# Order of rope products and of maxima blocks at a batch boundary of an attention and soft-MoE layer

## The reference

```python
h = _layernorm(x, axis=-1) * (1 + ca) + sa
x = x + ga * _L0_attn_ref(h, Wq, Wk, Wv, Wo)      # rope(q), rope(k), causal softmax
h = _layernorm(x, axis=-1) * (1 + cb) + sb
x = x + gb * _L0_ffn_ref(h, ...)
# in _L0_ffn_ref:
dispatch = jax.nn.softmax(logits, axis=1)          # over tokens
combine = jax.nn.softmax(logits.reshape(b, n, e * s), axis=-1)
slots = jnp.einsum('bnd,bnes->besd', xn, dispatch)
# two expert matmuls with a gelu between them, giving eo
out = jnp.einsum('bmd,bnm->bnd', eo, combine)
```

## Time and profile before

| | us |
|---|---|
| median of 3 runs | 3299.77 (3297.85 to 3300.67) |
| the profiled execution, device time | 3297.0 |
| its span, first to last instruction | 3295.2 |
| PE busy | 3071.7 (93%) |
| DVE busy | 2252.1 (68%) |
| ACT busy | 1763.6 (54%) |
| POOL busy | 329.8 (10%) |
| TensorE's granted clock, mean | 0.981 |

### The profile page before, as it was taken

How to read it: one execution, slowest core, us unless ns; L and a number is a source line. 1 busy time by engine, 2 the same in 40 slices (tenths; PEclk the granted TensorE clock), 3 DMA queues, 4 the chain that set the end, 5 groups by cost and what they waited for, 6 DMA issues and landing times.

```text
span 3295.2 us, 45435 instructions
## 1 busy us (share of the span) xinstructions
PE 3071.7 (93%) x17679; PEld 1544.8 (47%) x17679; DVE 2252.1 (68%) x4403; ACT 1763.6 (54%) x3199; POOL 329.8 (10%) x193
## 2 busy tenths in 40 slices
PE   5799999999889999998989999999997999999899
PEld 2433334447553333453854333344575433334468
DVE  4788887562678888756368888856546888885632
ACT  2366666564236666645514666654540566665560
POOL 3200000210400000111130000012122000002200
PEclk9799999999999999999999999999999999999999
DMA  4322201015502220002542202000443220100052
GB/s 129 99 40 40 40 2 39 14 52 197 149 20 40 40 40 27 20 7 95 190 119 46 39 9 40 27 20 7 151 163 103 40 41 11 31 27 27 9 179 81
DMA packets 123555, 201.89 MB, mean 61 GB/s; under 512 B 10094, under 2 KB 106996, under 8 KB 120232
## 3 DMA queue, kind: packets, MB, share of 16 engines
q1 hardware_dynamic: 110820, 148.58, 13.9%
q10 hardware_dynamic: 12520, 50.40, 8.2%
HBM read 156.01 MB, written 42.16 MB: 60 GB/s over the span
## 4 chain that ended last, share of the span: by engine, by line
PE 74%; DVE 17%; ACT 4%; issue 2%; POOL 1%; DMA 1%; ACTq 0%; SPq 0%; DVEq 0%; POOLq 0%
PE ps L694 14%; DVE pm L1269 12%; PE ps L674 10%; PE ps L614 9%; PE ps L795 7%; PE ps L850 7%; PE ps L627 6%; PE ps L881 3%; PE ps L870 3%; PE ps L574 2%; PE ps L738 2%; PE ps L659 2%; PE ps L678 1%; PE ps L808 1%; PE ps L603 1%
## 5 line engine op out<-in xcount | busy, mean ns | idle before, releaser
L1269 DVE TENSOR_REDUCE pm<-ps 128x1 f32<-128x512 f32 (+4 forms) x2560 | 1376.9, 602 | 273.6 <-PE ps L614 181.9
L983 ACT ACTIVATE R<-ps 128x512 f32<-128x512 f32 (+1 forms) x2240 | 1175.5, 593 | 603.0 <-PE ps L674 412.1
L674 PE MATMUL ps<-R 99*128 99x512 bf16 (+3 forms) x2560 | 827.9, 349 | 10.7 <-ACT R L983 6.0
L614 PE MATMUL ps<-R 96*128 96x512 bf16 x1536 | 578.6, 387 | 46.2 <-DVE pm L1269 40.7
L694 PE MATMUL ps<-R 128*17 128x512 f32 (+3 forms) x5120 | 528.9, 531 | 0.0
L614 PEld LDWEIGHTS ps<-R 96*128 96x128 bf16 x1536 | 147.3, 97 | 446.4 <-DVE pm L1269 372.0
L674 PEld LDWEIGHTS ps<-R 99*128 99x128 bf16 x2560 | 241.4, 97 | 146.0 <-ACT R L983 64.1
L694 PEld LDWEIGHTS ps<-R 128*17 128x17 f32 x5120 | 117.8, 96 | 280.1 <-issue 168.3
L850 PE MATMUL ps<-R 128*128 128x512 f32 x512 | 231.7, 610 | 14.0 <-ACT R L1050 13.9
L627 PE MATMUL ps<-R 128*128 128x257 f32 x1024 | 237.4, 388 | 4.1 <-ACT R L934 3.6
L795 PE MATMUL ps<-snT,R 128*128 128x512 f32 x512 | 230.1, 593 | 0.0
(11 more groups left out here) (151 smaller groups left out, 3321.7 us busy)
## 6 DMA issues: line engine op xcount, KB each, us to landing
R<-in_L_ffn_w_dram SPq DMA_DIRECT2D x64, 1024.0 KB, 5.8
R<-q_parts ACTq DMA_DIRECT2D x12, 768.0 KB
R<-k_parts ACTq DMA_DIRECT2D x12, 768.0 KB
R<-in_L_attn_x_dram SPq DMA_DIRECT2D x16, 512.0 KB, 8.4
q_parts<-R SPq DMA_DIRECT2D x16, 512.0 KB, 3.6
k_parts<-R SPq DMA_DIRECT2D x16, 512.0 KB, 3.4
R<-in_L_attn_x_dram SPq DMA_DIRECT2D x4, 2048.0 KB, 8.3
x_park<-R SPq DMA_DIRECT2D x16, 512.0 KB, 2.6
```

The lines of the kernel that those rows point to most:

```text
L614: last = mm(ps[:, bank, :], qt(4 * c + r), kt(4 * kc, 4), start=True, stop=True)
L674: last = mm(bank[:, i * w:(i + 1) * w], kst[g % 2][0:BROWS, h0 + i, j * P:(j + 1) * P], qst[g % 2][0:BROWS, h0 + i, (c + 1) * CH - w:(c + ...
L983: A(Eb[s % ESLOTS][:, h0:h0 + n, 0:w], ps[:, u % NST, 0:n * w].rearrange("p (n w) -> p n w", n=n), ACT.Exp, scale=SCALE).then_inc(s_ex, 1)
L1269: mx = lambda o, i: V.tensor_reduce(o, i, AX.X, ALU.max)
```

## The change

In `combine` on PE, a block now stands behind the expert products e = 0, 2, 4 and 6 of a tile, as many as the tile has, up to four; a fifth block stays behind the tile. `blocks_in_tile(n)` gives their numbers. On DVE the reductions of those blocks stand ahead of `out_tile(n)`, the fifth behind it; remainder 7 stays behind output tile 7. In the rope loop DVE's `products(b + 1, i)` moves ahead of `out_tile(i - 2)` and `remainder(b + 1, i - 1)`. The instructions themselves, their number and their operands stay the same.

```diff
--- before.py
+++ after.py
@@ -101,6 +101,11 @@
 
 def early_by(n):
     return EARLY * (n + 1 - FIRST_WITH_MAXES) // (NT - FIRST_WITH_MAXES)
+
+
+def blocks_in_tile(n):
+
+    return range(early_by(n - 1), min(early_by(n), early_by(n - 1) + E // 2)) if n >= FIRST_WITH_MAXES else range(0)
 
 
 def values_by(i):
@@ -626,7 +631,10 @@
                 for e in range(E):
                     last = mm(ps[:, 6 + n % 2, 0:D + 1], EcT[:, e, n * P:(n + 1) * P], eo[:, e, :],
                               start=e == 0, stop=e == E - 1)
-                last.then_inc(s_cm, 1)
+                    if e == E - 1:
+                        last.then_inc(s_cm, 1)
+                    elif b + 1 < B and e % 2 == 0 and e // 2 < len(blocks_in_tile(n)):
+                        max_unit(b + 1, blocks_in_tile(n)[e // 2])
 
             for c in range(NC):
                 turn_xhat(0, c)
@@ -903,6 +911,7 @@
                     m = 0
                     for n in range(QU - 2, NT):
                         combine(b, n)
+                        m += len(blocks_in_tile(n))
                         while m < early_by(n):
                             max_unit(b + 1, m)
                             m += 1
@@ -1526,14 +1535,17 @@
                     products(b + 1, 1)
                     remainder(b + 1, 0)
                     for i in range(2, QU):
+                        products(b + 1, i)
                         out_tile(i - 2)
                         remainder(b + 1, i - 1)
-                        products(b + 1, i)
                     m = 0
                     for n in range(QU - 2, NT):
+                        for m in blocks_in_tile(n):
+                            reduce_unit(b + 1, m)
                         out_tile(n)
                         if n == QU - 1:
                             remainder(b + 1, QU - 1)
+                        m = max(early_by(n - 1), 0) + len(blocks_in_tile(n))
                         while m < early_by(n):
                             reduce_unit(b + 1, m)
                             m += 1
```

## The result

The changed kernel takes 3240.8 us (median of 4 runs, 3237.0 to 3244.1) where the kernel before, run beside it, takes 3300.0 (3297.9 to 3300.7). The ratio is 0.9827, with an interval of 0.9815 to 0.9839: 59 us less. The forecast was 3240 us.

The account below looks back on a forecast made before the run. At three batch boundaries PE mostly waits for DVE; 0.5 + 9 x 3.47 + 9.6 + 1.0 + 0.5 + 1.4 = 44.2 us each saves 60.0 us, 3297.0 to 3237, median 3240 us. Forecast range 3230 to 3246 (0.66); 8 in 10: 3226 to 3262.

Parts of the forecast that it names:

- 44.2 us a stretch: Each batch boundary, combine tile 7's start to first `values` matmul: 44.2 us forecast, against 63.68, 64.21 and 64.69 before.
- Rope order: Rope units at the boundaries: products run at PE's pace, 6.92 us; products 7 end at 875.2, ending PE's 2.69 us wait.
- The term behind it: Combine tile 7 waits for output tile 5, now behind products 7, until 876.5: 0.5 us a boundary.
- Combine tiles and blocks: PE's work from combine 7 on: nine tiles of 3.47 us, 9.6 us of blocks, plus 1.0 us a boundary for insertions.
- The second rival: Blocks inserted within tiles show their weight loads, 0.29 us each, 31 us back: 3271 us, or 3255 for half; chance 0.09.
- DVE stays under PE: In the boundary stretch DVE has some 38.3 us of work against PE's 41 to 42.
- The 0.5 us that I took for tile 8: In tile 8 the fourth block waits for a reduction that stands behind remainder 7: 0.5 us a boundary.
- The first rival: DVE becomes the bound and PE waits inside tiles 7 to 10: 2 to 4 us a boundary, 3246 to 3252 us; chance 0.13.
- The end: `values` 0 waits for output tile 15, now behind four reductions and the tile's last matmul: 1.4 us a boundary.
- Full clock: Whole boundary stretch at 2.4 GHz, granted clock 1.00 instead of 0.92, since the two long PE waits are gone.
- What follows moves up whole: After the boundary, `values`, scores and maxima keep their order; their loads are issued some ten microseconds or more early.
- The slower rival: Park loop: late parks hold products at DVE's head; binds from 4.3 us landing, 3305 to 3310 us at 14; chance 0.04.

Follow-up runs that it names:

- after_third: The changed kernel run unaltered once more, as the reference beside the last variants: 3239.7 us, 0.9822 against the kernel before.
- both_waits: Changed kernel, but first `values` matmuls wait only for output tile 14, second group for 15, and output tile 5 precedes products 7 on DVE: 3232.3 us.
- after_again: The changed kernel run unaltered again beside other variants: 3239.7 us, 0.9830 against the kernel before.
- rope_only: Kernel before with only products moved ahead of output tile and remainder on DVE; blocks and reductions as before: 3283.4 us, 0.9961.
- order_only: Changed kernel with its rope and DVE order, but PE's blocks stand behind the tile again, as before: 3256.7 us, 0.9880 against the kernel before.

## Why the prediction was right

It named the place, the mechanism and the size: 44.2 us a stretch against 44.45 measured, 60.0 us in all against 59. That the stretch agrees to 0.25 us is in part luck: one term was 0.7 us too small and another 0.5 too large, as follows.

- Rope order: right. Products run at 6.91 us, products 7 are done at 876.1, which is 875.2 counted from combine tile 0 of the kernel before, and their wait is gone. The term behind it was too small: combine 7 waits for output tile 5 until 878.24 and not until 877.5 by the same clock, 1.2 us with latency against 0.5. The prediction let that tile end 1.3 us after products 7 (875.2 to 876.5), which is about what it takes alone (1.06 by the earlier trace rows) and a latency; by the 1.65 us that the prediction itself gives for a tile beside POOL the term would have been 0.8 or more. Here it ends 2.1 us after them, since its last step takes 1.44 us beside POOL's rotate. The stretch of 43.7 us in after_third, where it took 0.42, shows that it is this step.
- Combine tiles and blocks, 31.2 and 9.6 us: right. both_waits has no wait and takes 41.79 us, so 0.94 us are left over for the 36 insertions, 26 ns each if all of it is theirs. 1.0 was taken. The tiles take 4.5 to 4.9 us, where 4.3 to 4.8 were forecast. The second rival, weight loads in the open at 0.29 us, falls with its reason: if both loads were in the open, the full block of 0.22 us would take 0.5. By the rule of the Trainium skill (TensorE: Matmul & The Clock Gate, "Part 3: Packing small matmuls — row/col tiling") that the prediction cites, a weight load overlaps running matmuls only for other rows of the array; this trace does not agree, as the load at 894.87 shows. The same section also lets a load for the background weight buffer be pulled ahead, without that condition; whether these loads go there the profile doesn't show.
- DVE stays under PE: right. The 0.5 us that I took for tile 8 did not come; PE waits for no reduction. The first rival would have shown waits of L608 to L619 inside the tiles; there are none in tiles 7 to 15. DVE is busy for 38.7 us of the stretch (38.3 forecast), though a remainder beside POOL takes 2.28 us and not 2.06.
- The end, 1.4 us: 1.18 of wait and 0.2 of latency.
- Full clock: right, 1.00 in all three stretches.
- What follows moves up whole: right; from `values` 0 to the next logits 470.4 us after and 470.6 before, in batch 1.
- The slower rival: its loop is as described, 11.72 us a unit at two sets, and at three it costs nothing, as forecast. But it stands nearer to binding than the 2.1 us of slack that the prediction gave it: the landing of 2.2 us was read from one park, and for unit 2 it is 3.4 to 3.6 us in the changed kernel's profile. At the third boundary of after_again it is 4.3 us, and products 5 come 0.1 us late (2433.13, 7.04 behind products 4); at that of after_third it is 4.5, and they come 0.4 late. The prediction's 4.3 us, from which the loop would bind, agrees with that.

Where I was wrong was in the expectations of the parts. For the rope order alone I gave 24 us and measured 13: the first reduction still comes 1.7 us later than I had reckoned, since the remainder that was moved back stands in its way, and I took the low clock to vanish with a shorter wait. In the whole change neither matters, because blocks and reductions stand ahead of these and no long wait is left. The sum was right for the whole; the share that I gave the rope order was not.

## What to carry to other kernels

Where two engines take turns in tiles, look at what the second one does while the first works on the tile: here DVE waited 2.2 us a tile for its end with reductions at hand that needed only a few matmuls, and it was enough to put small pieces of work between the matmuls of a long accumulation, at some 26 ns each here, and their consumers ahead of the tile's own. Put the instruction that starts another engine's chain ahead of the one that waits for that chain's end, and check the buffers' loop first, with the slowest landing in the trace and not one row's: with one set fewer the same order was slower than the kernel before. The gains of the two parts alone (13.4 and 36.6 us) did not add up to the whole (57): reckon with what each leaves for the other to wait on.

## What the runs showed of the hardware

The granted clock doesn't follow from a wait's length alone. In rope_only the same wait of 3.0 us (2.99, 3.00, 3.00) was followed by a combine tile of 3.70, 6.15 and 4.97 us, and in order_only the same wait of 1.86 us by full clock once and by the low clock twice. And it can fall with no long wait near: the first row is 12 us in batch 3's attention of the changed kernel, the second 12 us in batch 0's attention of after_again.

```profile
2824.00:2836.00 12.00, 10.77 (x60) 2.98 (x60) 7.32 (x20) 5.52 (x11) 0.00 (x0) 0.86 0.01 2
```

```profile
472.00:484.00 12.00, 10.78 (x60) 2.87 (x59) 8.38 (x19) 6.60 (x13) 0.00 (x0) 0.86 0.00 1
```

Rows of the same stages in the profile of before are all at 1.00. Such a fall costs 2 to 3 us (batch 3's attention took 473.3 us in the changed kernel's profile, and 471.3, 470.4 and 470.6 in those of before, after_again and after_third, which have none there). Eight of the ten profiles have one or two of them in an attention stage, before and rope_only none, and four have one in the row from 468 to 480. The kernel alone doesn't decide it, since the three profiles of the changed kernel differ; what brings them on is open. They are likely a part of the spread of runs, 7 us from 3237.0 to 3244.1: the mean granted clock is 0.986 in the fastest of the four and 0.983 in the slowest. To judge 1 us a boundary, the stretches in the trace are the better measure: 44.44, 44.47 and 44.45 us.
